# Last norm of a mixture-of-experts tail: when the sorted table is cleared, how far bias reads run ahead, and powers taken in pairs

## The reference

```python
for e in range(NUM_EXPERTS):
    h = jax.nn.gelu(x_flat @ w1[e] + b1[e], approximate=False)
    y = h @ w2[e] + b2[e]
    sel = expert_idx == e
    out = out + jnp.where(sel, expert_w, 0.0)[:, None] * y
...
x = _layernorm(x + _L0_attn_ref(x, ...), axis=-1)
x = _layernorm(x + _L0_xattn_ref(x, ctx_1024, ctx_1024), axis=-1)
x = _layernorm(x + _L0_ffn_ref(x, ...), axis=-1)
```

## Time and profile before

| | us |
|---|---|
| median of 3 runs | 201.72 (200.91 to 202.88) |
| the profiled execution | 203.06 |
| its span, first to last instruction | 201.3 |
| PE busy | 175.7 (87%) |
| DVE busy | 123.8 (61%) |
| ACT busy | 97.0 (48%) |
| Pool busy | 68.7 (34%) |
| mean granted clock of TensorE | 0.975 |

### The profile page before, as it was taken

How to read it: one execution, slowest core, us unless ns; L and a number is a source line. 1 busy time by engine, 2 the same in 40 slices (tenths; PEclk the granted TensorE clock), 3 DMA queues, 4 the chain that set the end, 5 groups by cost and what they waited for, 6 DMA issues and landing times. The chain is left out here.

```text
span 201.3 us, 11917 instructions
## 1 busy us (share of the span) xinstructions
PE 175.7 (87%) x5244; PEld 153.5 (76%) x5244; DVE 123.8 (61%) x363; ACT 97.0 (48%) x264; POOL 68.7 (34%) x129
## 2 busy tenths in 40 slices
PE   0998996999999999739999999999899969899940
PEld 0986884767666769639899888999799759899940
DVE  0232798499998280235899893242579803988881
ACT  2422882569787446412343343322245617566750
POOL 6180000557565300000000001810226740689884
PEclk9999999999999999985999999999999999999996
DMA  5944000000000000000000000005960858787300
GB/s 178 373 125 141 7 0 0 0 10 3 0 3 0 3 3 7 3 3 3 0 0 0 2 2 0 7 3 165 352 101 26 250 144 224 200 215 234 97 8 4
DMA packets 15632, 14.57 MB, mean 72 GB/s; under 512 B 1350, under 2 KB 12001, under 8 KB 15603
## 3 DMA queue, kind: packets, MB, share of 16 engines
q1 hardware_dynamic: 14867, 13.10, 23.1%
q0 software_dynamic: 736, 1.06, 1.5%
HBM read 12.08 MB, written 2.53 MB: 73 GB/s over the span
## 5 line engine op out<-in xcount | busy, mean ns | idle before, releaser
L564 PE MATMUL banks<-V 32*32 32x64 f32 x1664 | 37.6, 231 | 6.0 <-issue 4.3
L564 PEld LDWEIGHTS banks<-V 32*32 32x32 f32 x1664 | 33.7, 107 | 8.6 <-issue 7.9
L570 PE MATMUL banks<-MM,WT 32*32 32x64 f32 x1536 | 35.8, 233 | 0.0
L570 PEld LDWEIGHTS banks<-MM,WT 32*32 32x32 f32 x1536 | 30.8, 107 | 0.0
L1154 DVE SCALAR_TENSOR_TENSOR MM<-V,banks 128x512 f32<-128x512 f32 x24 | 16.5, 686 | 18.1 <-PE banks L564 17.6
L949 ACT ACTIVATE V<-banks 128x512 f32<-128x512 f32 x20 | 11.9, 597 | 24.4 <-PE banks L570 24.4
L387 POOL MEMSET WT<- 128x1950 f32 x1 | 1.7, 1723 | 57.5 <-PE banks L570 57.5
L1019 ACT ACTIVATE GG<-banks,b1T 128x128 f32<-128x128 f32 x60 | 16.9, 378 | 5.6 <-PE banks L848 5.6
L848 PE MATMUL banks<-qkl,GG 128*128 128x128 f32 x120 | 15.9, 277 | 2.5 <-DVE qkl L1400 1.8
L848 PEld LDWEIGHTS banks<-qkl,GG 128*128 128x128 f32 x120 | 14.5, 192 | 3.1 <-DVE qkl L1400 2.0
L827 PE MATMUL banks<-E,GG 128*128 x120 | 16.3, 279 | 0.5 <-ACT GG L1019 0.5
(11 more groups left out here) (217 smaller groups left out, 401.0 us busy)
## 6 DMA issues: line engine op xcount, KB each, us to landing
GG<-in_L_ffn_w SPq DMA_DIRECT2D x15, 256.0 KB
wqkv<-in_L_attn_w_qkv SPq DMA_DIRECT2D x3, 512.0 KB, 5.3
Tt<-padded_taps SPq DMA_DIRECT2D x1, 1024.0 KB, 5.7
sorted_tokens<-WT SPq DMA_DIRECT2D x1, 975.0 KB, 13.5
GG<-in_L_ffn_b SPq DMA_DIRECT2D x15, 64.0 KB
WT<-sorted_tokens SPq DMA_DIRECT2D x1, 585.0 KB, 4.6
x_sb<-in_x SPq DMA_DIRECT2D x1, 512.0 KB, 4.0
wfc<-in_L_attn_w_fc SPq DMA_DIRECT2D x1, 512.0 KB, 6.9
```

Source lines behind the costliest of these rows:

```text
L564: return mm(bank[PV_BANKS[k % RING]][quad(q), 64 * n:64 * n + 64], V[quad(q), g, 0, :], V[quad(q), g], start=True, stop=True)
L570: return mm(bank[QM_BANKS[k % RING]][quad((q + 2) % 4), 64 * n:64 * n + 64], Q[quad(q), g, :], MM[quad(q), g], start=True, stop=True)
```

## The change

The clear of the table is issued on SP before the wait for the value products and the load of `w2`. `sort_rows` waits for each batch's own rows, not for the last of its group. SP reads four expert numbers at once after the second routing step and issues `w1` of blocks 4 to 7 before it waits for `xs_sent` (before: 4 and 5), and `b2` of 4 to 7 behind the three loads. `yt` has eight buffers. Three blocks get their deviation on ACT (before: two). The powers of blocks 2 and 3, 4 and 5, 6 and 7 are taken as pairs, one instruction each. On PE down 2 comes before the transposes of 4 and 5, which stand together, and up 4 and up 5 follow each other. DVE reads biases two blocks ahead up to block 9, then one ahead.

```diff
-POWERS = NB - 2
-SKEW = 4
+POWERS = NB - 3
+YT_SLOTS = 8
+DEVIATIONS = {0: ((0, 1), (1, 2)), 2: ((2, 4),), 4: ((4, 6),), 6: ((6, 8),), 7: ((8, 9),), 8: ((9, 10),),
+              9: ((10, 11),), 10: ((11, 12),)}
...
             sp.dma_start(gw[:], gate_w).then_inc(in_gate, 16)
+            sp.wait_ge(xs_zero, 1)
+            sp.dma_start(slot_rows(xs_dram), xs).then_inc(xs_cleared, 16)
             sp.wait_ge(U_mm, B)
             sp.dma_start(w2s, w2.rearrange("e (k p) d -> p e k d", k=FK)).then_inc(in_ffn, 16)
-            sp.wait_ge(xs_zero, 1)
-            sp.dma_start(slot_rows(xs_dram), xs).then_inc(xs_cleared, 16)
...
             sp.wait_ge(expert_ready, 2)
-            experts += expert_numbers(mybir.EngineType.SP, EARLY, EARLY + 2)
-            for j in range(EARLY, EARLY + 2):
+            experts += expert_numbers(mybir.EngineType.SP, EARLY, W1_SLOTS)
+            for j in range(EARLY, W1_SLOTS):
                 first_weights(j)
             sp.wait_ge(xs_sent, 16 * B)
             for n, (lo, hi) in enumerate(LOADS):
                 sp.dma_start(xs[:, lo:hi, :], slot_rows(xs_dram)[:, lo:hi, :]).then_inc(xs_loaded[n], 16)
-            for j in range(EARLY, EARLY + 2):
+            for j in range(EARLY, B2_SLOTS):
                 second_bias(j)
...
             def sort_rows(n, lo, hi):
-                pool.wait_ge(x2_ready, hi)
                 pool.wait_ge(weight_ready, n + 1)
                 pool.wait_ge(slot_ready, n + 1)
                 for b in range(lo, hi):
+                    pool.wait_ge(x2_ready, b + 1)
...
+            def slot_deviations(lo, hi):
+
+                pool.wait_ge(slot_var, hi)
+                nc.gpsimd.tensor_tensor(stat("rstd", lo, hi - lo), stat("sd", lo, hi - lo),
+                                        stat("mhalf").broadcast_to([P, hi - lo]), ALU.pow).then_inc(slot_rstd, hi - lo)
+
             for j in range(NB):
-                if j + 1 < POWERS:
-                    slot_deviation(j + 1)
+                for lo, hi in DEVIATIONS.get(j, ()):
+                    slot_deviations(lo, hi)
...
+            up(0)
+            up(1)
+            up(2)
+            down(0)
+            up(3)
+            down(1)
+            down(2)
+            pe.wait_ge(expert_ready, 2)
+            experts += expert_numbers(mybir.EngineType.PE, EARLY, EARLY + 1)
+            tokens_transposed(NS)
+            tokens_transposed(NS + 1)
+            down(3)
+            up(NS)
+            for j in range(NS + 1, NB):
+                up(j)
+                experts += expert_numbers(mybir.EngineType.PE, j, j + 1)
+                if j + 1 < NB:
+                    tokens_transposed(j + 1)
+                down(j - 1)
+            down(NB - 1)
...
             with_bias(0)
+            with_bias(1)
+            read = 2
+            rows_loaded(0)
+            rows_loaded(1)
             for j in range(NB):
...
                 weighted(j)
                 settle()
-                if j < NB - 1:
-                    spread(j)
-                if j >= 1:
+                ended = [g for g in groups if g[1] == j]
+                for lo, hi in ended:
+                    if hi - lo == 2:
+                        normed(lo)
+                        normed(lo + 1)
+                if j > POWERS:
                     normed(j - 1)
-            spread(NB - 1)
+                spread(j)
+                for lo, hi in ended:
+                    if hi - lo == 1:
+                        normed(lo)
+                while read <= min(NB - 1, j + 2 if j < 8 else j + 1):
+                    with_bias(read)
+                    read += 1
             normed(NB - 1)
```

More of the change, by code:

```diff
@@ L148, in program @@
         hT = gg_flat[:, 4096:4096 + 3 * F].rearrange("p (s c) -> p s c", s=3)
-        yt = gg_flat[:, 5632:5632 + 4 * D].rearrange("p (s d) -> p s d", s=4)
+        yt = gg_flat[:, 7168:7168 + YT_SLOTS * D].rearrange("p (s d) -> p s d", s=YT_SLOTS)
         b2b = gg_flat[:, 6144:6144 + B2_SLOTS * D].rearrange("p (s d) -> p s d", s=B2_SLOTS)
@@ L319, in _ @@
                 sp.dma_start(xs[:, lo:hi, :], slot_rows(xs_dram)[:, lo:hi, :]).then_inc(xs_loaded[n], 16)
-            for j in range(EARLY, EARLY + 2):
+            for j in range(EARLY, B2_SLOTS):
                 second_bias(j)
-            for j in range(EARLY + 2, NB):
+            for j in range(B2_SLOTS, NB):
                 experts += expert_numbers(mybir.EngineType.SP, j, j + 1)
@@ L833, in _, with up @@
             pe.wait_ge(in_ffn, 16)
[L834 to L856, removed]
+            def up(j):
+                if j < NS:
+                    pe.wait_ge(xsT_early[j // 2], 1)
+                else:
+                    pe.wait_ge(xsT_ready, j - NS + 1)
+                pe.wait_ge(w1_in[j % W1_SLOTS], 16 * (j // W1_SLOTS + 1))
+                if j >= 3:
+                    pe.wait_ge(h_ready, FK * (j - 2))
+                for k in range(FK):
+                    i = mm(bank[j % 3][:, P * k:P * k + P], w1b[:, j % W1_SLOTS, P * k:P * k + P], xsT[:, j, :],
+                           start=True, stop=True)
+                i.then_inc(up_mm, 1)
+            up(0)
[18 more added lines that the diff above has]
+            down(NB - 1)
         @block.scalar
@@ L1364, in with_bias @@
                 dve.wait_ge(b2_in[j % B2_SLOTS], 16 * (j // B2_SLOTS + 1))
-                if j >= 4:
-                    dve.wait_ge(ys_ready, j - 3)
-                v.tensor_tensor(yt[:, j % 4, :], bank[4 + j % 2][:, 0:D], b2b[:, j % B2_SLOTS, :], ALU.add
+                if j >= YT_SLOTS:
+                    dve.wait_ge(ys_ready, j - YT_SLOTS + 1)
+                v.tensor_tensor(yt[:, j % YT_SLOTS, :], bank[4 + j % 2][:, 0:D], b2b[:, j % B2_SLOTS, :], ALU.add
                                 ).then_inc(down_read, 1)
@@ L1377, in weighted @@
             def weighted(j):
-                row = yt[:, j % 4, :]
+                row = yt[:, j % YT_SLOTS, :]
                 step(v.scalar_tensor_tensor(out=row, in0=row, scalar=xs[:, j, D:D + 1], in1=xs[:, j, 0:D],
@@ L1382, in spread @@
             def spread(j):
-                step(v.bn_stats(stat("bn", 6 * j, 6), yt[:, j % 4, :]))
+                step(v.bn_stats(stat("bn", 6 * j, 6), yt[:, j % YT_SLOTS, :]))
                 settle()
@@ L1387, in spread @@
                 v.tensor_scalar(stat("sd", j, 1), stat("mv", 2 * j + 1, 1), EPS, None, ALU.add).then_inc(slot_var, 1)
+            groups = [g for j in sorted(DEVIATIONS) for g in DEVIATIONS[j]]
             def normed(j):
                 if j < POWERS:
-                    dve.wait_ge(slot_rstd, j + 1)
+                    dve.wait_ge(slot_rstd, [hi for lo, hi in groups if lo <= j < hi][0])
                 else:
@@ L1395, in normed @@
                     settle()
-                v.tensor_scalar(ys[:, j, :], yt[:, j % 4, :], stat("mv", 2 * j, 1), stat("rstd", j, 1),
+                v.tensor_scalar(ys[:, j, :], yt[:, j % YT_SLOTS, :], stat("mv", 2 * j, 1), stat("rstd", j, 1),
                                 ALU.subtract, ALU.mult).then_inc(ys_ready, 1)
```

## The result

The changed kernel takes 206.62 us (median of 4 runs, 205.78 to 207.51), beside 202.3 us for the kernel before on the same chip: ratio 1.0213, interval 1.0124 to 1.0302. It is slower, as forecast, but by 4.3 us in place of 2.3, and 206.62 lies above the range. The profiled execution took 207.51 us with a span of 204.8, against 201.3 before.

What follows compares the result with a forecast made beforehand. The last stretch ends on Pool, with PE and DVE close behind. Pool's rounds +1.8, first pair +0.2, sort -0.1 and loads +0.4 give +2.3 us on the 201.72 median: 204.0 us, 8-in-10 range 201.0 to 205.5.

Steps and rivals of the forecast that it cites:

- Pool's rounds: Pool from scatter 0 to scatter 14: 25.9 us against 24.07 before, so +1.8 us, bounds +1.3 to +2.7.
- The pair round: Pool's rounds before scatters 2, 4, 6: scatter, pair power, DVE's norm, then 0.91 us lead; 3.08 us, three times.
- Rival B: Pool prepares the scatter while waiting, lead 0.19 instead of 0.91; pair round 2.36, total 202.4 us; chance 0.22.
- rival C: Both norms of a pair are ready when Pool comes, so only Pool's total work counts: 200.1 us or less; chance 0.15.
- rival D: Down products already ran one block behind and the clear was not waited for; only Pool's part is left; in the forecast.
- The +0.2 for the first pair: Norm 2 on DVE, behind bias 5 and weighted 4, starts after pair (2, 4) is ready: +0.2 us, bounds 0 and 1.0.
- The loads: Two more `w1` issues and 512 KB ahead of SP's loads of sorted rows delay them: +0.4 us, bounds 0 and +1.4.
- rival A: The loads of sorted rows stand behind the weights in SP's queue: +1.4 in place of +0.4, 205.0 us; chance 0.13.
- The upper bound in the prediction: Loads of sorted rows can't pass the weights in SP's queue, by ring order: +1.4 us.
- The third root: Block 12's root on ACT makes DVE wait; last scatter starts at 198.7, +0.7 against before, under Pool's +2, adding 0.
- PE with gaps after block 8: Sign that the forecast is right: PE waits for DVE's bias reads after block 8; no size given.
- The clear and the sort: Earlier clear on SP worth 0; each batch waiting for its own rows -0.1 us, bounds 0 and -0.4.

Runs made afterwards that it cites:

- e1: Changed kernel with every power taken singly, one scatter ahead as in the kernel before: 202.69 us, ratio 1.0105 to the kernel before.
- e5: Changed kernel with its three pairs of powers each issued one scatter earlier: 203.78 us, ratio 1.0065 to the kernel before.
- g3: f2 with the change's pairs of powers and nothing else: 205.11 us, ratio 1.0169 to the kernel before.
- f2: f1 with block 12's power back on Pool, so two roots on ACT: 202.45 us, ratio 1.0013 to the kernel before.
- e6: Kernel before with only the clear issued ahead of the value products' wait and `w2`: 202.03 us, ratio 0.9976.
- g1: e4 with two more 256 KB weight loads, copies that nothing reads, ahead of the loads of sorted rows: 204.39 us, ratio 1.0094 to the kernel before.
- e4: Kernel before with `w1` of blocks 6 and 7 issued ahead of the wait for sorted rows, `b2` of 4 to 7 behind the loads: 202.87 us, ratio 1.0083.
- g2: f2 with `w1` of blocks 6 and 7 ahead of the loads of sorted rows: 204.15 us, ratio 1.0043 to the kernel before.
- e2: Changed kernel with `w1` of blocks 6 and 7 back behind the loads of sorted rows, pairs kept: 206.1 us, ratio 1.0239 to the kernel before.
- e7: e1 with the clear back behind `w2`: 204.04 us in 4 runs, ratio 1.0142 to the kernel before.
- f1: Changed kernel with single powers, `w1` of blocks 6 and 7 behind the loads, clear back behind `w2`: 203.25 us, ratio 1.006 to the kernel before.
- f3: Kernel before with blocks 0 to 3 loaded ahead of 4 and 5, and one wait a batch in the sort: 203.44 us, ratio 1.011.

## Why the prediction was right and wrong

**Pool's rounds: right.** The pair round was put at 3.08 us and is 3.06, three times; the pair's power at 0.73 and is 0.76. To scatter 12 the forecast's rounds make 23.24 us (25.9 less two of 1.33), measured 23.38. e1 takes the idle rounds away, e5, which only moves the pairs, takes most of the loss away, and g3 brings it back alone. Rival B (the lead before a scatter not paid) and rival C (Pool held by its total work) fell with it; rival D's two points hold, since the order (f2) and the clear (e6) gain nothing that can be told. The +0.2 for the first pair did not come: at 177.22 the pair stands directly behind its scatter. The runs put the price of the pairs at some 2.2 us (e1 against after) or 3.1 (g3 against f2), and the rounds explain 2.4; the intervals allow all of it.

**The loads: the failed size.** "I take +0.4" against +1.43 in the profile; rival A's +1.4 is met by the number. By the other profiles, however, the difference is some 0.5 on average (0.75 more in the scatters' landing, 0.26 less in the loads), within their spread, and the rest of the 1.43 is the spread of single executions: the size of +0.4 is not shown wrong on average, but its place was. Rival A's mechanism did not hold in after: the DMA engines were nearly idle when the loads had been issued (0.13 of 167 to 168 us), and the load of blocks 0 to 3 takes no longer behind more weights (4.31 us in g1 with 1 MB more ahead, 4.42 on average with none). In its place the weights move while the sort's last scatters do, and these land later. The rule that I cited from the Trainium skill, DMA: Bandwidth & Descriptors, section "Queues, rings and completion order", speaks of the order in which descriptors are taken within a queue. In after it had nothing left to hold; only in g1, with weights still moving at the issue, can it have held the first load. The upper bound in the prediction met the profiled +1.43 by luck; as far as the cost is shown, it sat one transfer earlier, in Pool's own DMAs. The times agree on its sign: e4 +0.8%, g2 +0.3%, not told apart from nothing in g2.

**The end: the failed step.** The third root "adds 0 now" in the prediction, and "PE with gaps after block 8" stands there without a price. The account of the roots took the last GELU as it was before (table load at 193.0) and moved only what stands behind it. The runs show +0.62 in its place, in two parts. 0.29 stand with three roots even where the clock stays at 1.00 (e1, e2, e7, f1): in e1 norm 13 ends only 0.34 us before Pool is free for its scatter, and the lead is 0.86. The other 0.33 come with the delay that the pair rounds hand on: the bias reads are late, PE stalls 1.93 us, the granted clock is 0.50, the table load comes at 195.22, and scatter 13 pays the whole lead, idle for 0.91 us. A floor has to be moved by the delays that feed it.

**The clear and the sort: right.** 0 in the span, and -0.12 for one wait a batch (-0.1 forecast): 38.14 us from memset to last scatter of the sort in e4 and e6, with the old wait, 38.00 in f3, with the new. What stands outside the span was not looked at; in after it is 1.0 over before in the profiled execution, and no more than before in the three others.

**The sum.** In the profile +3.9 against +2.3: the loads +1.0 too small, the end +0.6. By the runs the parts are: pairs 2.2 to 3.1 us, weights 0.6 to 1.7, third root 0 to 1, early clear 0 to 0.8; together 2.8 to 6.6, around the 4.3 measured, whose interval is 2.5 to 6.1. The range ended at 205.5 because both bounds were put on the median one at a time; even the loads' upper bound and the price of the end together make only 205.6. Of the last 1.0, 0.6 is the base: the forecast was put on 201.72, the median of three runs, and the kernel before has 202.3 with the fourth. The other 0.4 is the profiles' own spread: the profiled execution of before was 0.8 over this median, that of after had the span of its kernel's median (204.8), and the stages in front gave 0.4 back. Both are well inside the interval. The early clear is no part of it: the time outside the span is 1.7 us in the three executions of after that were not profiled.

## What to carry to other kernels

Batching small instructions on one engine can save time (here a power of two columns took 0.76 us, two of one column 1.17), but a batch needs the last of its inputs before its first output can start. Where the order of before keeps every wait over early, that costs more than it saves (here 1.32 us idle for 0.4 us of power). Where it pays to batch, the batch's place decides: the same three pairs one scatter earlier brought the loss from 2.1% to 0.7% (e5). A load issued "into the gap" before a join can delay the transfer that the join waits for, though it goes through another queue (here 0.75 us on average): look at what is still landing then. And treat a term from one profiled transfer as a draw: here the same load took 3.4 to 5.1 us.

## What was not expected of the hardware

PE's waits for the sorted rows were followed by a lower granted clock in some executions and not in others: after waits of 2.05 us (e4), 2.09 (e6) and 2.60 (f3) the products that followed ran at 1.2 GHz for over 2 us, while after 1.72 (after), 0.99 (e1) and 0.72 (f2) the clock stayed at 1.00. The length of the wait alone doesn't tell: behind a bias read PE stood 1.93 us in after and 2.12 in g3, and the clock fell, but 2.10 us in e2, and it stayed at 1.00. The timeline of PE in e4, and its windows:

```profile
168.04 0.33 PE L820 MATMUL banks<-ident,WT 128*128 128x128 f32 x1 [2.05 <-DMA WT<-sorted_tokens]
168.24 1.15 PE L827 MATMUL banks<-E,GG 128*128 x8
169.23 1.87 PE L848 MATMUL banks<-qkl,GG 128*128 128x128 f32 x8
```

```profile
168.00:170.00 2.00, 1.96 (x13) 0.82 1.08 304
170.00:172.00 2.00, 2.00 (x12) 0.50 1.07 256
```

Eight matmuls cost 1.87 us there in place of 1.06, just where the first output blocks are made. A late load is thus paid twice, which may be why e4 costs more in time (0.8%, 1.7 us) than its landing shows; no run separates the two.
